# A new order of the beginning of a transformer-layer kernel: loads, norm chain, ternary weights and the second batch's transposes

## What is computed

```python
x = x + attn(layernorm(x), w_q, w_k, w_v, w_o)     # softmax(q k^T / sqrt(16)) v, then w_o
x = x + ffn(layernorm(x), w_gate, w_up, w_down)
# bitlinear: w_mean = mean|w|; w_q = clip(round(w/(w_mean+eps)), -1, 1); w_eff = w_q*w_mean*scale
# xq = int4_quant(x); inter = int8_quant(up * relu(gate)^2); out = bitlinear(inter, w_down)
```

## Time and profile before

| | us |
|---|---|
| median of 3 runs | 1126.78 |
| lowest, highest | 1121.69, 1143.36 |
| the profiled execution | 1124.7 |
| its span (first to last instruction) | 1122.7 |

### The profile page before, as it was taken

The page is one execution under the profiler, slowest core; times in us unless marked ns, Lnnn a source line. Parts: engine busy times, 40 slices in busy tenths (PEclk is TensorE's granted clock), DMA queues, the critical chain, the costliest instruction groups (busy, mean ns, idle before and its releaser), DMA issues.

```text
span 1122.7 us, 17288 instructions
## 1 busy us (share of the span) xinstructions
PE 961.9 (86%) x5917; PEld 292.8 (26%) x5932; DVE 901.5 (80%) x1561; ACT 789.4 (70%) x1436; POOL 183.6 (16%) x291
## 2 busy tenths in 40 slices
PE   1734899999999999999999999999888669888886
PEld 1411322222222222222222222211111135444453
DVE  4469888888888888889888988899993168888874
ACT  3642327888888888888888888888889446566664
POOL 2379000101101021012010210110001011111210
PEclk9976989999999999999999999999999989999998
DMA  9330001102111111110210111211343331111110
GB/s 359 106 93 19 2 1 39 57 21 48 38 49 49 34 36 47 52 34 20 68 47 20 48 51 37 48 34 43 104 140 86 109 106 39 39 37 37 47 38 29
DMA packets 37987, 64.83 MB, mean 58 GB/s; under 512 B 3606, under 2 KB 18966, under 8 KB 37654
## 3 DMA queue, kind: packets, MB, share of 16 engines
q1 hardware_dynamic: 37910, 63.85, 19.2%
HBM read 42.27 MB, written 21.23 MB: 57 GB/s over the span
## 4 chain that ended last, share of the span: by engine, by line
PE 54%; DVE 22%; issue 8%; ACT 7%; DMA 2%; POOL 2%; SPq 0%; DVEq 0%; POOLq 0%; ACTq 0%
PE ps L412 17%; PE ps L355 14%; DVE mx L897 11%; PE ps L333 8%; PE ps L391 7%; PE ps L297 3%; ACT PB L651 2%; PE ps L475 2%; DVE PB L807 2%; DVE hm L980 2%; ACT OS L657 1%; ACT nmT L662 1%; POOL rstd L1175 1%; PE ps L453 1%; PE ps L497 1%
## 5 line engine op out<-in xcount | busy, mean ns | idle before, releaser
L897 DVE TENSOR_REDUCE mx<-ps 128x1 f32<-128x512 f32 x1024 | 642.8, 683 | 77.1 <-PE ps L355 77.1
L651 ACT ACTIVATE PB<-ps 128x512 f32<-128x512 f32 x1024 | 560.0, 595 | 126.0 <-PE ps L391 119.5
L355 PE MATMUL ps<-QK 48*128 48x512 f16 x1024 | 295.0, 388 | 59.3 <-DVE mx L897 59.2
L391 PE MATMUL ps<-QK 50*128 50x512 f16 x1024 | 291.4, 383 | 6.9 <-ACT PB L651 6.1
L412 PE MATMUL ps<-PB,Vg 128*32 128x512 f32 x2048 | 273.6, 606 | 0.7 <-ACT PB L651 0.7
L355 PEld LDWEIGHTS ps<-QK 48*128 48x128 f16 x1024 | 75.6, 93 | 402.3 <-DVE mx L897 328.5
L333 PE MATMUL ps<-XV,wqk 128*128 128x512 f16 x384 | 112.4, 389 | 13.8 <-ACT nmT L662 13.7
L1104 POOL TENSOR_SCALAR nmb<-nm 128x16 f16<-128x16 f32 x32 | 6.5, 204 | 608.9 <-DVE nm L902 608.9
L475 PE MATMUL ps<-tu,Vg 128*128 128x344 bf16 x256 | 49.1, 315 | 24.1 <-DVE XV L969 24.0
L412 PEld LDWEIGHTS ps<-PB,Vg 128*32 128x32 f32 x2048 | 40.3, 108 | 106.6 <-ACT PB L651 89.5
L453 PE MATMUL ps<-wo,XV 128*128 128x512 f32 x128 | 61.8, 627 | 6.0 <-DVE PB L926 5.3
(11 more groups left out here) (132 smaller groups left out, 756.0 us busy)
## 6 DMA issues: line engine op xcount, KB each, us to landing
parts_d<-spl SPq DMA_DIRECT2D x64, 128.0 KB
att_d<-OS SPq DMA_DIRECT2D x32, 256.0 KB
PB<-x SPq DMA_DIRECT2D x28, 256.0 KB, 2.7
QK<-parts_d SPq DMA_DIRECT2D x48, 128.0 KB, 4.6
QK<-parts_d SPq DMA_DIRECT2D x16, 256.0 KB, 4.3
XV<-att_d SPq DMA_DIRECT2D x2, 2048.0 KB, 8.3
QK<-rden_d SPq DMA_DIRECT2D x8, 512.0 KB, 7.5
out<-PB SPq DMA_DIRECT2D x16, 256.0 KB, 2.0
```

Of the source, the lines that this page charges most:

```text
L355: nc.tensor.matmul(ps[:, at % S_BANKS, :], QK[rows, sup % 2, 2 * set_ + p, 0, half * HALF + qt * P:half * HALF + (qt + 1) * P], QK[rows, s ...
L391: nc.tensor.matmul(ps[:, T_BANK + n % T_BANKS, :], QK[rows, sup % 2, 2 * set_ + p, 1, kt * P:(kt + 1) * P], QK[rows, sup % 2, 2 * set_ + p ...
L651: nc.scalar.activation(PB[:, at % 3, 2 * (i % 2) + i // 2, :], ps[:, T_BANK + n % T_BANKS, :], ACT.Exp, scale=exp_reg).then_inc(probs, 1)
L897: nc.vector.tensor_reduce(mx[:, v % 2, idx, kh:kh + 1], ps[:, at % S_BANKS, :], AX.X, ALU.max).then_inc(s_used, 1)
```

## The change

In words, stream by stream:

- **SP**: all eight tiles of the first batch are loaded ahead of w_k, w_q and w_v (was: four tiles, w_k, w_q, four tiles, the scales, w_v).
- **Norm chain**: one per weight, in the order k, q, v (CHAIN), each with its own TensorE sum and PSUM bank. The chain of w_v stands between job 0 and job 1, behind the copies of all eight tiles.
- **VectorE**: statistics of tiles 4 to 7 are taken early; the tiles and weights are interleaved anew. tiles(2), the statistics and normalisations of tiles 8 to 11, now stands ahead of the low half of w_v. The clipping of w_gate goes from GpSimd to VectorE: two quarters ahead of the reductions, one after k = 1 and one after k = 3. What followed w_up's factor moves back some steps.
- **GpSimd**: the clipping of w_gate goes away; the memsets of Vg and of the aux rows and the two small identities go ahead of the first rstd.
- **ScalarE**: squares of w_k come first; w_v's high half comes later; w_gate's rounding goes behind all jobs, w_up's sums behind value copies 1 and 2, its rounding behind 4 and 5.
- **TensorE**: the mean of w_gate stands after all six jobs, that of w_up after value tile 4 (was 2). Tiles 8 to 11 are transposed ahead of value tile 8 and 12 to 15 ahead of value tile 10.

The diff, cut to its core:

```diff
-EARLY_TRANSPOSES = {7: 8, 9: 12}
+EARLY_TRANSPOSES = {8: 8, 10: 12}
+CHAIN = (1, 0, 2)
+NORM_BANK = (7, 6, 3)
...
-        def pe_norms(pe, w0, w1):
+        def pe_norm(pe, w):
+            pe.wait_ge(wn_sum, CHAIN.index(w) + 1)
+            nc.tensor.matmul(ps[:, NORM_BANK[w], w:w + 1], ones[:], sqsum[:, w:w + 1], start=True, stop=True)\
                 .then_inc(wn_psum, 1)
...
         def _(pe):
             pe.wait_ge(ident_ok, 1)
-            for t in range(4):
-                pe_tile_transpose(pe, t)
+            pe_tile_transpose(pe, 0)
+            pe_tile_transpose(pe, 1)
             pe.wait_ge(consts, 3)
-            pe_norms(pe, 0, 2)
+            pe_norm(pe, 1)
+            pe_tile_transpose(pe, 2)
+            pe_tile_transpose(pe, 3)
+            pe_norm(pe, 0)
...
-                if n == 1:
-                    pe_norms(pe, 2, 3)
+                if n == 0:
+                    pe.wait_ge(xt_copy, BT)
+                    pe.wait_ge(xl_ready, BT)
+                    pe_norm(pe, 2)
                 if n == 3:
...
-                    pe_mean(pe, 0)
+            pe_mean(pe, 0)
...
-                if t == 2:
+                if t == 4:
                     pe_mean(pe, 1)
...
         def _(act):
-            for t in range(4):
-                act_tile_copy(act, t)
+            act_squares(act, 1)
+            act_tile_copy(act, 0)
+            act_tile_copy(act, 1)
             act_squares(act, 0)
-            act_squares(act, 1)
+            act_tile_copy(act, 2)
+            act_tile_copy(act, 3)
             act_weights(act, 1, 0, 256)
...
-            act_weights(act, 2, 0, HID)
             act_job(act, 2)
             act_abs(act, 0, GATE_ORDER[2])
+            act_weights(act, 2, 0, HID)
+            act_job(act, 3)
             act_abs(act, 0, GATE_ORDER[3])
...
             act_job(act, 5)
-            act_round(act, 0, GATE_ORDER[2])
-            act_round(act, 0, GATE_ORDER[3])
+            act_round(act, 0, GATE_ORDER[0])
+            act_round(act, 0, GATE_ORDER[1])
             for t in range(TILES):
...
-                if t < 2:
-                    act_abs(act, 1, 2 * t)
-                    act_abs(act, 1, 2 * t + 1)
                 act_value_copy(act, t)
-                if t in (2, 3):
-                    act_round(act, 1, 2 * t - 4)
-                    act_round(act, 1, 2 * t - 3)
-                if t == 5:
+                if t == 0:
+                    act_round(act, 0, GATE_ORDER[2])
+                    act_round(act, 0, GATE_ORDER[3])
+                if t in (1, 2):
+                    act_abs(act, 1, 2 * t - 2)
+                    act_abs(act, 1, 2 * t - 1)
+                if t in (4, 5):
+                    act_round(act, 1, 2 * t - 8)
+                    act_round(act, 1, 2 * t - 7)
+                if t == 7:
                     act_weights(act, 0, 256, 256)
...
         def _(dve):
-            dve_tiles(dve, 0)
             for t in range(4):
-                dve_tile_rest(dve, t)
-            dve_scales(dve, 0, 2)
-            dve_weights(dve, 1, 0, 256, 1)
-            for t in range(4, BT):
                 dve_bn(dve, t)
+            dve_stats(dve, 0)
+            dve_bn(dve, 4)
+            dve_bn(dve, 5)
+            for t in range(4):
+                dve_normalise(dve, t)
+            dve_bn(dve, 6)
+            dve_bn(dve, 7)
             dve_stats(dve, 1)
+            dve_total_squares(dve, 1)
+            dve_tile_rest(dve, 0)
+            dve_tile_rest(dve, 1)
             dve_normalise(dve, 4)
             dve_normalise(dve, 5)
-            dve_weights(dve, 0, 0, 256, 2)
+            dve_scales(dve, 1)
+            dve_total_squares(dve, 0)
+            dve_tile_rest(dve, 2)
+            dve_tile_rest(dve, 3)
             dve_normalise(dve, 6)
             dve_normalise(dve, 7)
-            for t in range(4, BT):
-                dve_tile_rest(dve, t)
+            dve_weights(dve, 1, 0, 256, 1)
+            dve_scales(dve, 0)
+            dve_tile_rest(dve, 4)
+            dve_tile_rest(dve, 5)
+            dve_weights(dve, 0, 0, 256, 2)
+            dve_tile_rest(dve, 6)
+            dve_tile_rest(dve, 7)
+            dve_total_squares(dve, 2)
+            dve_scales(dve, 2)
             dve_exp_scale(dve)
-            dve_scales(dve, 2, 3)
             dve_v_back(dve)
+            dve_tiles(dve, 2)
             dve_weights(dve, 2, 0, HID, 3)
...
             dve_weights(dve, 1, 256, 256, 4)
-            dve_tiles(dve, 2)
+            dve_ternary(dve, 0, GATE_ORDER[0], 0)
+            dve_ternary(dve, 0, GATE_ORDER[1], 1)
...
-                if k == 1:
+                if k in (1, 3):
+                    dve_ternary(dve, 0, GATE_ORDER[2 + k // 2], 2 + k // 2)
+                if 5 <= k < 9:
+                    dve_bn(dve, k + 7)
+                if k == 9:
+                    dve_stats(dve, 3)
+                if k == 11:
                     dve_total(dve, 1)
                     dve_factor(dve, 1)
-                if 4 <= k < 8:
-                    dve_bn(dve, k + 8)
-                if k == 8:
-                    dve_stats(dve, 3)
-                if 9 <= k < 13:
-                    dve_ternary(dve, 1, k - 9, k - 9)
-                if k == 16:
-                    dve_weights(dve, 0, 256, 256, 5)
-                if k == 19:
+                if k in (14, 16, 18, 20):
+                    dve_ternary(dve, 1, (k - 14) // 2, (k - 14) // 2)
+                if k == 23:
                     for t in range(8, 12):
                         dve_tile_rest(dve, t)
                         dve_normalise(dve, t + 4)
                 if k == 27:
+                    dve_weights(dve, 0, 256, 256, 5)
+                if k == 31:
...
-            rstds(0)
...
+            g.memset(Vg[:, :, :, :, :], 1.0).then_inc(vg_ones, 1)
             g.memset(crow[:, 0, :], AUX_HIGH).then_inc(aux_set, 1)
             g.memset(crow[:, 1, :], AUX_LOW).then_inc(aux_set, 1)
-            norm_root(2, 3)
-            for job in range(JOBS_AHEAD):
+            rstds(0)
+            rstds(1)
...
+            norm_root(1)
+            norm_root(0)
+            pool_split_job(pool, 0)
+            norm_root(2)
+            for job in range(1, JOBS_AHEAD):
                 pool_split_job(pool, job)
-            g.memset(Vg[:, :, :, :, :], 1.0).then_inc(vg_ones, 1)
             rstds(2)
-            for order, q in enumerate(GATE_ORDER):
-                pool_ternary(pool, 0, q, order)
             rstds(3)
...
             tiles(0)
+            tiles(1)
             weights(1)
             weights(0)
-            tiles(1)
+            weights(2)
             for n, s in enumerate((s_gate, s_up, s_down)):
...
-            weights(2)
```

More of the change, by code:

```diff
@@ L305, in pe_mean @@
             if w == 0:
-                pe.wait_ge(wn_tot, 2)
+                pe.wait_ge(wn_tot, 3)
             elif w == 1:
@@ L310, in pe_mean @@
                 .then_inc(w_psum, 1)
-        def pe_norms(pe, w0, w1):
-            pe.wait_ge(wn_sum, w1)
-            nc.tensor.matmul(ps[:, (6, 3)[w0 // 2], w0:w1], ones[:], sqsum[:, w0:w1], start=True, stop=True)\
+        def pe_norm(pe, w):
+            pe.wait_ge(wn_sum, CHAIN.index(w) + 1)
+            nc.tensor.matmul(ps[:, NORM_BANK[w], w:w + 1], ones[:], sqsum[:, w:w + 1], start=True, stop=True)\
                 .then_inc(wn_psum, 1)
@@ L614, in act_weights @@
         def act_weights(act, w, c, n):
-            act.wait_ge(wn_scale, w // 2 + 1)
-            act.wait_ge(wn_sum, w + 1)
+            act.wait_ge(wn_scale, CHAIN.index(w) + 1)
+            act.wait_ge(wn_sum, CHAIN.index(w) + 1)
             nc.scalar.activation(wpart[w][:, 0, :, c:c + n], wraw[w][:, :, c:c + n], ACT.Copy, scale=wscale[:, w:w + 1])\
@@ L636, in act_round @@
             if wsum_first(w, q):
+                act.wait_ge(consts, 3)
                 act.wait_ge(w_fac, w + 1)
@@ L831, in dve_factor, with dve_total_squares, dve_scales @@
             nc.vector.reciprocal(wrec[:, w:w + 1], wrec[:, w:w + 1]).then_inc(w_fac, 1)
[L833 to L839, removed]
-                .then_inc(wn_step, 1)
[L841 to L845, removed]
+        def dve_total_squares(dve, w):
+            c = CHAIN.index(w)
+            dve.wait_ge(wn_psum, c + 1)
+            nc.vector.tensor_scalar(sqtot[:, w:w + 1], ps[:, NORM_BANK[w], w:w + 1], 1e-30, None, ALU.max).then_inc(wn_tot, 1)
+        def dve_scales(dve, w):
+            c = CHAIN.index(w)
+            own = qkscale[:, w:w + 1]
+            dve.wait_ge(wn_pow, c + 1)
+            nc.vector.tensor_scalar(own, rnorm[:, w:w + 1], HALF_RANGE / float(np.sqrt(HID)), None, ALU.mult)\
+                .then_inc(wn_step, 1)
+            dve.wait_ge(wn_step, 2 * c + 1)
+            nc.vector.tensor_scalar(own.bitcast(I32), own.bitcast(I32), EXPONENT, None, ALU.bitwise_and).then_inc(wn_step, 1)
+            dve.wait_ge(wn_step, 2 * c + 2)
+            nc.vector.tensor_scalar(wscale[:, w:w + 1], own, W_SCALE, None, ALU.mult).then_inc(wn_scale, 1)
```

(13 more changed lines are left out.)

12 lines of the change are left out of this document (3 added, 9 removed).

## The result

The changed kernel takes 1117.78 us (median of 8 runs, 1115.34 to 1120.14) against 1126.7 of the kernel before. The ratio is 0.994, 95% interval 0.9917 to 0.9962. The profiled execution took 1115.34 (span 1113.5). The kernel before has single runs near 1143 (2 of these 8, 12 of all 41 taken in this study); the ratio leaves them out, and they turn out to matter. The prediction was 1095, with a range of 1086 to 1107.

What follows compares the result with a forecast made beforehand. The bound was the TensorE and VectorE chain of waits, weak from 68.5 to 126.4 us, where GpSimd passes stretch VectorE's. Values ending at 128.3 instead of 158.8 take 30.5 off 1124.7: 1094, median forecast 1095, range 1086 to 1107.

Steps and rivals of the forecast that it cites:

- Parts 1 to 4: Loads and norm chain up to the values: job 0 at 22.2 us, split 1 done 32.7, splits 51.5, values 58.6.
- rival (a): Six splits: the parts' trips to memory and back take twice as long, +10.8 us, giving 1106; chance 0.07.
- Parts 5 and 6: From the values on: first reduction at 67.6 us, VectorE resumes at 99.4, values end at 128.3, first exponential 134.5.
- Part 6: Remaining value tiles after VectorE resumes: one tile fewer left, 30.8 us instead of 34.2, ending at 128.3.
- Rival (b): Value tiles 2 to 7: TensorE stays at 1.2 GHz, +15 us, giving 1110; chance 0.06.
- the sum: Whole kernel: values end at 128.3 instead of 158.8, so 30.5 us come off the profiled 1124.7, giving 1094.
- Rival (d): Attention locks in another phase: 1.5 us a unit over 32 units, giving 1142, slower than before; chance 0.03.

Runs made afterwards that it cites:

- fill: The changed kernel with two unused matmuls of 512 columns added in each of steps 16 to 31 of the last superunit; 1102.8 us.
- push6: The changed kernel with one transposed-score matmul of superunit 2 issued 6 times more; 1120.54 us.
- push10: The changed kernel with one transposed-score matmul of superunit 2 issued 10 times more; 1104.19 us.
- push12: The changed kernel with one transposed-score matmul of superunit 2 issued 12 times more; 1121.84 us.
- norm_late: The changed kernel with the normalisations of tiles 8 to 11 moved behind reduction k = 3, their statistics left in place; 1102.31 us.
- ternary_alone: The kernel before with only w_gate's clipping moved from GpSimd to VectorE, behind the second low half of w_k; 1119.78 us.

## Why the prediction was wrong

**Parts 1 to 4 held.** Job 0 at 21.57 (22.2 forecast); split 1 done at 31.78 (32.7); the third rstd at 53.45 (53.0); the low half of w_v 2.35 (2.4); values at 58.48 (58.6), as late as foretold. The six splits' trips took 20.2 instead of 18.8, so rival (a) had 1.4 us in it. The rule of the port pair in the Trainium skill (SBUF — State Buffer, "SBUF: two separate sides"), by which a low half beside an idle GpSimd is 2.4 rather than 3.27, agrees with the row of 2.35.

**Parts 5 and 6 were 3.4 us short.** The first reduction came at 66.79 (67.6), and VectorE was done with the rests and normalisations behind k = 23 at 99.7 (99.4): its sum was 1.1 us short, most of which the early start hid. But TensorE, waiting for VectorE at the transposes, got the low clock near 95 us (two tiles' transposes 2.14, six matmuls 2.72), and VectorE resumed at 102.46, after 2.79 of waiting. Part 6 had given the transposes no low clock. First exponential 137.94, forecast 134.5. Rival (b) had named this cost for half tiles 2 to 7. It didn't come in this profile, but it came for one or two half tiles near 81 us in fill, push6, push10 and push12, and they were 6.4 to 7.5 us behind the forecast, not 3.4.

**The start of the attention took 1.7 more**: 27.0 at the first exponential, 25.3 at the first sums. TensorE is at the low clock there from 136 to 150 us, in the kernel before from 163 to 173.

**The step that failed is the sum.** "1124.7 - 30.5" takes all that follows the first exponential as unchanged. Its instructions are; its clock isn't. 16.6 us are lost in the last two units. Rival (d) said that the attention may run otherwise when it starts elsewhere, and put the price on every unit; 29 of the 31 distances between the copies disproved that, and the price sat in the last two, where TensorE has gaps. The terms add up: 3.4, 1.7 and 16.6, less 0.5 gained behind the attention, are the 21.2 us by which the profiled execution (9.3 us faster, not 30.5) missed the sum. What I passed over was in sight: the runs before spread from 1121.69 to 1143.36, 22 us, where a kernel that always does the same had no reason to. The last unit of its profile, with TensorE busy 13.66 of 17.12 us, was the place to ask.

## What to carry to other kernels

- When a kernel's runs come in two groups, look for the stretch whose clock differs before you forecast anything that shifts it. The gain of an edit and the toss of the clock are of one size here (25 and 17 us), and by an estimate from these two an edit of 25 can look worth 9 or 42.
- Hold the clock (two spare matmuls a step in a stretch where TensorE waits for ScalarE), then measure edits against each other.
- One profile of a kernel whose clock varies is one draw: the same beginning put the first exponential at 137.94 to 142.00.
- GpSimd's long SBUF passes cost VectorE's normalisations and ternary passes beside them (0.54 to 5.12 us, 0.52 to 5.03), not its PSUM reductions (0.67) nor its statistics (0.68): either move the work or move what stands beside it.

## What the runs showed of the hardware

- The granted clock falls from 2.4 to 1.2 GHz in a unit that TensorE works through as in the kernel before (the one ahead of it: busy 20.95 of 24.67 us), with gaps of 0.15 to 0.68 us. It stays down for 51 us in which TensorE is busy over 90% (24.16 of 26.78, 24.76 of 27.06), since the same work takes longer. The Trainium skill (TensorE: Matmul & The Clock Gate, "HAM oscillation — how this bites in real kernels") tells of such falls for idle gaps of microseconds, and in "A second HAM failure mode: psum-queue depth-cycling" of short idles between groups of matmuls. The trace agrees with the second and not with the first: no gap in the ten microseconds ahead of the fall is above 0.68 us.
- The same stream of instructions keeps the clock or loses it from one execution to the next: the kernel before lost it in 12 of 41 runs by their times, and in the traces a fall at the same matmuls lasted three microseconds in norm_late and 61 in ternary_alone. 32 more matmuls of 512 columns (two took 0.61 us) kept it in 18 of 18 runs of three kernels, three of them seen in traces.
- One GpSimd pass with two operations over 1376 columns takes 4.85 us, the same on VectorE 0.87 (fp32 in) or 0.52 (bf16 in), and the second 5.03 beside GpSimd. It goes the other way too: in norm_late a GpSimd pass that takes 0.62 alone takes 2.51 beside VectorE's low half of w_v (2.35).
